# A mixture-of-experts stage on one core: the second projection turned to float32r over 512 tokens and summed in PSUM, the routing weights applied before it

## The reference, cut to what matters

```python
shared = relu(xt @ sW1 + sb1) @ sW2 + sb2
probs = softmax(xt @ router_W + router_b)              # 15 experts
top_p, top_i = top_k(probs, 3)
cw = zeros((n, 15)).at[arange(n)[:, None], top_i].set(top_p)
h = relu(einsum('nd,edh->neh', xt, eW1) + eb1)
ye = einsum('neh,ehd->ned', h, eW2) + eb2
return shared + einsum('ned,ne->nd', ye, cw)
```

## Time and profile before

| | |
|---|---|
| three runs | 2200.13, 2201.32 and 2196.71 us, median 2200.13 us |
| profiled execution, first to last instruction | 2195.9 us; no time of its own is given apart from the three runs, which lie 0.8 to 5.4 us above its span |
| busy share | PE 88%, DVE 77%, ACT 47%, POOL 22% |
| mean granted clock of PE | 0.948 |
| stage ffn0a | 242.3 to 474.1 us |
| stage ffn0b | 541.6 to 771.4 us |
| stage ffn1a | 1052.2 to 1284.0 us |
| stage ffn1b | 1962.0 to 2192.7 us |

### The profile page before, as it was taken

One profiled execution on the slowest core, in us unless ns is written; L12 is line 12 of the kernel. 1 busy time (PEld: TensorE's weight loads), 2 busy tenths in 40 slices (PEclk: granted clock), 3 DMA queues, 4 the chain that ended last, 5 costly groups with the idle time before them and its releaser, 6 DMA issues. The chain is left out here.

```text
span 2195.9 us, 35701 instructions
## 1 busy us (share of the span) xinstructions
PE 1937.5 (88%) x12178; PEld 1438.1 (65%) x12178; DVE 1695.5 (77%) x5509; ACT 1035.0 (47%) x1617; POOL 492.2 (22%) x558
## 2 busy tenths in 40 slices
PE   5886799998999967673799979999999999989999
PEld 3554699986899923332799965555555555549998
DVE  6997788876888879998688877766767767738887
ACT  3442244433444434442444444666666665554443
POOL 1110100012000022230200024534544543330000
PEclk8998999999999988876899989999999999999999
DMA  3000100000000010000000000000000000000000
GB/s 100 6 5 4 56 1 1 1 1 1 1 1 1 1 40 1 0 1 0 1 1 1 1 1 1 1 1 1 1 1 1 1 1 1 1 1 11 11 9 13
DMA packets 17638, 15.73 MB, mean 7 GB/s; under 512 B 4209, under 2 KB 16177, under 8 KB 16946
## 3 DMA queue, kind: packets, MB, share of 16 engines
q1 hardware_dynamic: 15152, 12.66, 1.8%
q10 hardware_dynamic: 2306, 0.78, 0.2%
HBM read 10.55 MB, written 2.88 MB: 6 GB/s over the span
## 5 line engine op out<-in xcount | busy, mean ns | idle before, releaser
L2205 ACT ACTIVATE soft_prob<-psum 128x1024 f32<-128x1024 f32 (+3 forms) x384 | 302.4, 812 | 203.8 <-PE psum L2085 202.2
L2297 DVE TENSOR_REDUCE soft_mx<-psum 128x1 f32<-128x512 f32 (+2 forms) x352 | 231.0, 688 | 116.1 <-PE psum L2155 79.3
L2155 PE MATMUL psum<-soft_own,soft_stack 128*128 128x512 f32 (+3 forms) x768 | 249.3, 376 | 24.5 <-DVE soft_mx L2293 10.7
L163 POOL TENSOR_TENSOR norm_rstd<-norm_mv,s_const_minus_half 128x4 f32<-128x4 f32 x64 | 65.2, 1019 | 915.0 <-DVE norm_mv L158 908.4
L2085 PE MATMUL psum<-soft_stack,soft_own 128*128 128x512 f32 (+3 forms) x768 | 225.4, 377 | 2.8 <-POOL soft_stack L2062 2.2
L2085 PEld LDWEIGHTS psum<-soft_stack,soft_own 128*128 128x128 f32 x768 | 125.3, 189 | 133.2 <-issue 81.6
L2293 DVE CUSTOM_DVE_ANT_0 psum<-psum,s_soft_sel 128x384 f32<-128x384 f32 (+1 forms) x256 | 157.4, 639 | 64.8 <-PE psum L2155 64.0
L2155 PEld LDWEIGHTS psum<-soft_own,soft_stack 128*128 128x128 f32 x768 | 139.8, 193 | 92.7 <-DVE soft_mx L2297 42.9
L1075 DVE SCALAR_TENSOR_TENSOR x<-psum,ffn1b_cw,x 128x128 f32<-128x128 f32 x512 | 144.1, 344 | 29.7 <-PE psum L949 20.9
L2102 PE MATMUL psum<-soft_prob,soft_v_pad 128*32 128x512 f32 (+3 forms) x1536 | 163.6, 498 | 3.5 <-ACT soft_prob L2205 2.1
L1075 DVE SCALAR_TENSOR_TENSOR x<-psum,ffn1a_cw,x 128x128 f32<-128x128 f32 x512 | 144.2, 344 | 27.2 <-PE psum L949 18.1
(11 more groups left out here) (381 smaller groups left out, 4114.0 us busy)
## 6 DMA issues: line engine op xcount, KB each, us to landing
s_ffn_w<-in_ffn_w SPq DMA_DIRECT2D x4, 1024.0 KB, 7.8
out_x<-x SPq DMA_DIRECT2D x8, 256.0 KB, 2.3
x<-in_x SPq DMA_DIRECT2D x4, 384.0 KB, 8.0
mamba_coef_dram<-mamba_out_coef SPq DMA_DIRECT2D x8, 96.0 KB, 1.6
s_ret_w<-in_ret_w SPq DMA_DIRECT2D x1, 640.0 KB, 3.5
x<-in_x SPq DMA_DIRECT2D x4, 128.0 KB, 3.5
s_ret_cos<-in_ret_cos SPq DMA_DIRECT2D x1, 512.0 KB, 7.0
s_ret_sin<-in_ret_sin SPq DMA_DIRECT2D x1, 512.0 KB, 7.3
```

The source lines that it names most:

```text
L163: self.nc.gpsimd.tensor_tensor(self.rstd[:, :], self.mv[:, :, 1], self.const["minus_half"][:, 0:GT], ALU.pow).then_inc(self.rstd_ready, 1)
L2155: ins = pe.matmul(per_head[:, n, :], stack[:, u % HT, i * P:(i + 1) * P], own[:, u % 3, g, half * BLK:half * BLK + width], start=(n == 0), ...
L2205: nc.scalar.activation(prob[:, done % PROBS, :, low(n):BLK], e_ps[:, n % 2, :, low(n):BLK], ACT.Exp, scale=float(HD) ** -0.5).then_inc(exp ...
L2297: nc.vector.tensor_reduce(mx[:, i, half, heads.start:heads.stop], bank[:, 0:width * len(heads)].rearrange("p (g k) -> p g k", k=width), AX ...
```

## The change

It touches `ffn_stage` alone (and the list of tiles kept between ffn0a and ffn0b, which now has w2's parts too).

- The second projection is computed with the experts' w2 stationary and 512 token columns moving, in three float32r passes (w2_high h_high, w2_low h_high, w2_high h_low). All 16 experts and the bias term add up in one PSUM bank for each block. The sum is channel-major, so ACT copies it to SBUF (`yt`), PE transposes it back (`back`, 4 transposes) and DVE adds it to `x` in one instruction (`add`).
- The routing weight therefore goes in before the second projection: `weigh` on DVE computes (h_ps + b1) * cwb for 15 experts of each block, where `cwb` holds the weight of each token on all 128 partitions. ACT applies relu to that and writes it as float32r (`high`); for ten experts of 16 it writes it a second time in float32 (`full`) and POOL computes low = full - high; for the six in ON_VECTOR DVE computes low.
- `cwb` comes through DRAM: the transposed weights are copied to SBUF (`cwx`), SP writes them to `cw_dram`, waits for that, and loads 15 pieces of 2 KB, each broadcast to 128 partitions (256 KB a load), into a ring of 20.
- `h_ps` has four banks; PE runs `down` four experts behind `up` (LAG).
- In the stages with `split=True` POOL makes low parts of w2 too (six instructions in place of three) and ACT the high part of w2, all of it ahead of POOL's first `invert`.

Its core:

```diff
+H_BANKS = 4
+T_RING, HIGH_RING, FULL_RING = 4, 6, 3
+LAG = 4
+PIECE, PIECES_KEPT = 1, 20
+ON_VECTOR = (2, 5, 7, 9, 12, 14)
...
+            def spread(q):
+                sp.wait_ge(cwx_ready, q + 1)
...
+                sp.dma_start(cw_dram[q % 2, :, :], cwx[EXACT:EXACT + E, :]).then_inc(stored, 16)
+                sp.wait_ge(stored, 16 * (q + 1))
+                for j in range(E // PIECE):
...
+                    sp.dma_start(cwb[:, k % PIECES_KEPT, :, :].rearrange("p e t -> p (e t)"),
+                                 src.to_broadcast([P, PIECE * BLK])).then_inc(piece_loaded[k % PIECES_KEPT], 16)
...
+            split_x(0)
             if split:
-                for i in range(len(W1_PIECES) - 1):
-                    low_w1(i)
-            blocks(body)
+                for which, i in ((0, 0), (0, 1), (1, 0), (0, 2), (1, 1), (1, 2)):
+                    low_weights(which, i)
+            norm.invert(pool, 1)
+            for g in range(BLOCKS):
+                for e in range(NE):
+                    if e not in ON_VECTOR:
+                        low_of(NE * g + e)
+                    if e == 3 and g + 1 < BLOCKS:
+                        split_x(g + 1)
+                    if e == 11 and g + 2 < more_blocks:
+                        norm.invert(pool, g + 2)
...
+            def down(n):
...
+                pe.matmul(y_ps[:, g % 2, :], w2_parts[0][:, e, :], high[:, slot, :], start=False, stop=False)
+                pe.matmul(y_ps[:, g % 2, :], w2_parts[1][:, e, :], high[:, slot, :], start=False, stop=False)
+                if e in ON_VECTOR:
+                    pe.wait_ge(low_vector, vector_lows(n))
+                else:
+                    pe.wait_ge(low_pool, pool_lows(n))
+                pe.matmul(y_ps[:, g % 2, :], w2_parts[0][:, e, :], low[:, slot, :], start=False, stop=(e == E))\
+                    .then_inc(down_done, 1)
...
+            pe.wait_ge(cw_one, 1)
+            route(0)
+            for n in range(EXPERTS):
+                g, e = divmod(n, NE)
+                up(n)
+                if n == H_BANKS - 1:
+                    transpose_cw(0)
+                if n >= LAG:
+                    down(n - LAG)
+                if e == 0 and g + 1 < more_blocks:
+                    tokens(g + 1)
+                if e == 3 and g + 1 < BLOCKS:
+                    route(g + 1)
+                if e == 6 and g:
+                    back(g - 1)
+                if e == 8 and g + 1 < BLOCKS:
+                    transpose_cw(g + 1)
...
+            for n in range(EXPERTS):
+                g, e = divmod(n, NE)
+                parts_of(n)
+                if e == 1 and g + 1 < more_blocks:
+                    copy_x(g + 1)
+                if e == 4 and g + 1 < BLOCKS:
+                    exp(g + 1)
+                if e == 5 and g:
+                    copy_y(g - 1)
+                if e == 8 and g + 1 < BLOCKS:
+                    copy_cwt(g + 1)
...
             shift(0)
             probabilities(0)
             largest(0)
-            combine_weights(0, 0)
+            combine_weights(0)
...
+            norm.statistics(dve, 1)
+            norm.scale(dve, 1)
+            for n in range(EXPERTS):
+                g, e = divmod(n, NE)
+                if e < E:
+                    weigh(n)
+                if e - 1 in ON_VECTOR:
+                    low_of(n - 1)
+                if e == 4 and g + 1 < BLOCKS:
+                    shift(g + 1)
+                if e == 5 and g + 1 < BLOCKS:
+                    probabilities(g + 1)
+                if e == 6 and g + 1 < BLOCKS:
+                    largest(g + 1)
+                if e == 7 and g + 1 < BLOCKS:
+                    combine_weights(g + 1)
+                if e == 8 and g:
+                    add(g - 1)
+                if e == 11 and g + 2 < more_blocks:
...
+                    norm.statistics(dve, g + 2)
+                if e == 13 and g + 2 < more_blocks:
+                    norm.scale(dve, g + 2)
+            add(BLOCKS - 1)
```

More of the change, by code:

```diff
@@ L953, in body @@
-            def body(g, p, more):
-                for e in range(2, NE, 2):
-                    up(g, p, e)
-                    up(g, p, e + 1)
-                    if e == 4 and (more or out is None):
-                        norm.transpose(pe, g + 1)
-                    down(g, p, e - 2)
-                    down(g, p, e - 1)
-                    if e == 2:
-                        transpose_cw(g, p)
-                    if more and e == 6:
-                        route(g + 1, 1 - p)
-                if more:
-                    up(g + 1, 1 - p, 0)
-                    up(g + 1, 1 - p, 1)
-                down(g, p, E - 1)
-                down(g, p, E)
@@ L1070, in add_expert @@
[L1070 to L1093 removed]
+                upper, lower = cw_parts[:, :, 0:NE], cw_parts[:, :, 32:32 + NE]
```

345 lines of the change are left out of this document (200 added, 145 removed).

## The result

The changed kernel runs in 2234.56 us (median of 4 runs, 2232.59 to 2237.61), beside 2198.89 us for the kernel before on the same chip (2196.71 to 2201.32): a ratio of 1.0162, 95% interval 1.0147 to 1.0178. It is 1.6% slower. The prediction was 2242 with a range of 2185 to 2300, and slower at 0.74.

A forecast was written before the change was run, and what follows sets the result against it. PE was taken to bound each block, before and after. Blocks of 26.5 us for 27.82 give back 42 us in 32 blocks, four dearer stage starts cost 84, so 42 more: 2242 us, range 2185 to 2300.

The forecast's parts named there:

- PE's sum: Steady block: PE's passes, bias, router, transposes and returns to float32r add up to 25.1 us, against 27.82 before.
- Waits inside a block: Steady block: PE waits 1.4 us at back, transpose_cw and route, ends 0.3 and 2.7, making a block 26.5 us.
- At 0.3 us each ... that is 5 us: Steady block: some 17 DVE instructions wait for POOL's port hold, 5 us in all, putting DVE at 24.5 us.
- without it I would put the waits below at 0.4 a block: Steady block: without the rule that POOL and DVE block each other's SBUF port, PE's waits would be 0.4 us.
- The start of ffn0b: Stage ffn0b: a chain from router to first load delays the first weigh; 24.8 us against 7.2, 17.6 more.
- The split stages: Starts of the three split stages: scale(1) also waits for POOL's queue; about 31 us each, 66 more together.
- DVE's small instructions get the port between them: Split-stage starts: DVE's small instructions run between POOL's weight lows, with scale at 16.2 us after the barrier.
- The loads: Steady block: 15 loads of 256 KB, each 2.3 us to landing, stay ahead of 1.65 us an expert, so hidden.
- About 0.8 us of all queues each by the store's size: Broadcast loads: each 256 KB load takes about 0.8 us of all DMA queues, judged by the store's size.
- The rings cover the bursts: Rival, whole kernel: waits of 0.3 us a block and starts costing 60 give 2183 us, faster; chance 0.17.
- DVE sets the pace: Rival, steady block: DVE waits in full for POOL's 12 instructions, 32.2 us a block, 2425 in all; chance 0.10.
- The loads set the pace: Rival, steady block: broadcast loads take 5.0 us each, a block 76, the kernel about 3800 us; chance 0.06.

The follow-up runs named there:

- d_short_low: Changed kernel with POOL's ten lows a block cut to 32 of 512 columns from each stage's third block (output wrong): 2210.07 us, ratio 1.0038.
- a_tokens: Changed kernel with PE's tokens(1) issued behind transpose_cw(0) at a stage's start: 2201.83 us, ratio 1.0004 to the kernel before.
- e_loads_twice: Changed kernel with every 256 KB broadcast load issued a second time into a spare tile: 2276.60 us, ratio 1.0353 to the kernel before.
- c_later: Changed kernel with routing chain, back and add one expert later, transpose_cw and copy_cwt two, on PE, ACT and DVE: 2264.12 us, ratio 1.0286.
- k_all: Changed kernel with lows reshared, split_x on DVE, starts reordered, back at 7, transpose_cw at 9, route at 4 in first blocks: 2178.69 us, ratio 0.9904.
- l_route4: k_all with PE's route at expert 4 in every block instead of the first alone: 2155.62 us, ratio 0.9787 to the kernel before.

## Why the prediction was right, and where its steps were off

- **PE's sum.** 25.1 us a block predicted, and 25.03 busy. But the prediction added distances of starts, and by these PE's sum is 24.6 (25.03 less three times 0.16; d_short_low gives the same, 24.71 less 0.16). It was 0.5 too high, since the 97 passes came 0.228 us apart for 0.232 (0.4), and a group of four transposes costs 0.36, not 0.49, where nothing is late (0.4), against which the router and the bias pass cost 0.1 more.
- **Waits inside a block.** 1.4 us predicted in `back`, `transpose_cw` and `route`; measured as idle time 0.55, 0.23 and 0.47, 1.25 in all, in these three places and no other, and 1.7 by distances. So a block of 26.28 for 26.5, 49 us back in 32 blocks for 42, is right in its places, and closer in size than its two terms, 0.5 too high and 0.3 too low: that much is luck.
- **What makes the waits.** The step "At 0.3 us each ... that is 5 us" was mis-sized: DVE is held 1.9 us a block, in two instructions and not in a little of 17, since the order of a block is the same each time and an instruction is either beside one of POOL's or not. The step "without it I would put the waits below at 0.4 a block" was right: without the two holds 0.29 us is left, 0.45 by distances. Two errors hid each other here too: DVE's own work was put 1.1 us too low (19.4 for 20.5), mostly since `weigh` runs 749 ns and 0.66 apart for the 0.60 of the earlier trace rows, and the hold 3.1 too high; 24.5 was forecast for DVE, 22.4 measured.
- **The start of ffn0b.** First `weigh` at 22.0 predicted, at 22.4 measured, and 24.4 beside eight blocks for 24.8. The chain held step by step: combine weights at 6.8 (7.0), scale ended at 10.5 (10.7), `transpose_cw` ended at 16.2 (16.7); only the first load took 3.5 us for 2.3. a_tokens shows the cause: PE's order with `tokens(1)` ahead of `transpose_cw(0)`.
- **The split stages.** 31 predicted, 32.2, 31.4 and 31.9 measured: right in size, with a wrong step in it. "DVE's small instructions get the port between them" is refuted: five of them were held in full, by 1.1, 0.9, 2.0, 1.1 and 2.1 us, statistics came at 14.4 us, after POOL's lows (13.9), and `invert` waited for DVE and not, as predicted, for POOL's own queue. The sum of this step is also rounded up: 16.2 and 14.1 are 30.3, not 31.
- **The loads.** Hidden in steady blocks, as predicted, though each took 6.4 us to landing and not 2.3; e_loads_twice shows room for twice the bytes. "About 0.8 us of all queues each by the store's size" doesn't follow from the earlier trace rows, whose two stores differ by 0.7 us for 160 KB, or 1.1 for 256; it was right all the same, 256 KB at the 311 GB/s of e_loads_twice being 0.84. An estimate of 11.7 us a load stood beside this, from the Trainium skill, SBUF — State Buffer, section "A bandwidth-pool intuition that's wrong (but worth ruling out)"; the trace disagrees with taking a row that way: these loads of one 2 KB row to 128 partitions moved 152 GB/s in the block, and up to 311 when doubled.
- **The other engines.** POOL is busy 57% of a block for some 60; ACT has 17.8 us for 17, its relus 0.62 to 0.63 us alone and 0.52 in a row, no bound. `weigh` was free of the port, as taken.
- **The sum.** 84 less 42 predicted, 86 less 49 measured: 37 for 42, and the time 7 us under the forecast. The mechanism is the one forecast, a start that is paid four times; the closeness of the number owes something to errors that offset each other inside the block.
- **The rivals.** "The rings cover the bursts" failed on the start, as the prediction's break-even had it (waits of 1.25 against the 0.1 that it allowed). "DVE sets the pace" did not occur in the changed kernel; c_later, with 3.6 us held, is as near as any run came, at 27.9 and not 32. "The loads set the pace" did not occur.

What stays open: why the granted clock falls behind some of k_all's waits of 1.06 us and not behind others, nor behind the longer ones of c_later; whether PE's or DVE's order put the 0.29 us at `transpose_cw`; and what would take away the four small waits left in l_route4.

## What to carry to other kernels

Cost the start of a pipeline as a chain of its own, once for each time it is entered: an order that is right in the steady state (`tokens` at expert 0) can hold the chain at the entry, and four entries cost more here than 32 cheaper blocks gave. Where POOL and DVE share operands in SBUF, look for the pairs of instructions that lie beside each other in each repeat, not for a mean: two pairs made 1.0 of the 1.25 us of stalls. Sharing the work out anew, two indices and `split_x` on DVE, removed both, but at the price of a new hold of 0.5 us and of 0.7 us more work on DVE. When stalls are removed one at a time, watch that they don't gather into one long one.
